# Second close of a four-stage transformer: last unit in halves, gate products in fp32r parts, clamps on GpSimd

## The reference

```python
# third stage, its end: out is the attention's output
gated = out @ w_gate + b_gate            # 256 -> 512
a, g = jnp.split(gated, 2, axis=-1)
x = x + a * jax.nn.sigmoid(g)
# fourth stage
y = _layernorm(x)
x_q = jnp.clip(y / input_scale, -448.0, 448.0)
x_dq = x_q.astype(jnp.float8_e4m3fn).astype(x.dtype) * input_scale
w_dq = weight_fp8 * weight_scale
x = x + jnp.einsum('bsi,oi->bso', x_dq, w_dq) + bias
```

## Time and profile before

| | |
|---|---|
| median of 3 runs | 2159.44 us (2157.16 to 2160.05) |
| profiled execution | 2158.82 us, its span 2157.1 us |
| PE / DVE / ACT / POOL busy in the span | 91% / 55% / 64% / 37% |
| second close | from about 2050 us to the end of the span |
| granted TensorE clock, mean | 0.95 |

### The profile page before, as it was taken

The page is one execution under the profiler, slowest core; times in us unless marked ns, Lnnn a source line. Parts: engine busy times, 40 slices in busy tenths (PEclk is TensorE's granted clock), DMA queues, the critical chain, the costliest instruction groups (busy, mean ns, idle before and its releaser), DMA issues. The chain is left out here.

```text
span 2157.1 us, 37876 instructions
## 1 busy us (share of the span) xinstructions
PE 1965.9 (91%) x12227; PEld 1132.6 (53%) x12227; DVE 1179.3 (55%) x2115; ACT 1384.8 (64%) x1585; POOL 804.5 (37%) x706
## 2 busy tenths in 40 slices
PE   6989999999956599999999999958899999999897
PEld 5722333323232488888888888857622222222255
DVE  5511163534557723323333333337599999999967
ACT  5689999999933233233233233226599999999943
POOL 2001010111120241443342444211078888988922
PEclk9989999999965699999999999979899999999999
DMA  6753243442210530202202220238944425463011
GB/s 207 232 97 69 46 102 59 107 71 60 59 41 0 195 128 29 87 29 83 91 28 85 89 84 26 86 115 300 300 67 106 94 53 117 59 151 63 27 63 70
DMA packets 76964, 203.63 MB, mean 94 GB/s; under 512 B 13092, under 2 KB 28262, under 8 KB 74664
## 3 DMA queue, kind: packets, MB, share of 16 engines
q1 hardware_dynamic: 67048, 179.26, 31.0%
q0 software_dynamic: 6816, 18.62, 2.5%
q10 hardware_dynamic: 2896, 3.16, 0.5%
HBM read 338.84 MB, written 60.03 MB: 185 GB/s over the span
## 5 line engine op out<-in xcount | busy, mean ns | idle before, releaser
L1291 PE MATMUL psum<-A_qa,A_ka 50*128 50x512 f32 x2048 | 417.7, 473 | 26.6 <-DVE A_qa L1375 7.3
L1291 PEld LDWEIGHTS psum<-A_qa,A_ka 50*128 50x128 f32 x2048 | 177.5, 186 | 476.9 <-DVE A1f_probs L1385 243.3
L2475 PE MATMUL psum<-e_w_high,e_xT 128*128 x1136 | 386.9, 402 | 3.9 <-DVE e_xT L2425 3.8
L1509 POOL TENSOR_TENSOR A1f_probs<-A1f_probs,A1f_bias 128x512 f32<-128x512 f32 x256 | 327.3, 1290 | 83.0 <-ACT A1f_probs L1343 82.6
L1331 ACT ACTIVATE A0f_probs<-psum 128x1024 f32<-128x1024 f32 x256 | 337.1, 1317 | 8.6 <-PE psum L1291 5.4
L1343 ACT ACTIVATE A0f_probs<-psum 128x1024 f32<-128x1024 f32 x256 | 338.5, 1322 | 0.0
L1385 DVE SCALAR_TENSOR_TENSOR A1f_probs<-psum,A1f_bias 128x1024 f32<-128x1024 f32 x256 | 311.7, 1218 | 24.0 <-PE psum L1291 20.7
L2432 DVE TENSOR_TENSOR e_hT<-psum,e_hT 128x1024 fp32r<-128x1024 f32 x71 | 87.0, 1225 | 421.3 <-ACT e_hT L2396 421.3
L1310 PE MATMUL psum<-A1f_probs,v 128*32 128x512 f32 x2048 | 274.4, 607 | 17.3 <-POOL A1f_probs L1509 15.8
L1335 ACT ACTIVATE A1f_probs<-A1f_probs 128x1024 f32<-128x1024 f32 x256 | 273.9, 1070 | 4.7 <-DVE A1f_probs L1385 3.8
L1310 PE MATMUL psum<-A0f_probs,v 128*32 128x512 f32 x2048 | 273.6, 606 | 0.0
(11 more groups left out here) (291 smaller groups left out, 2746.6 us busy)
## 6 DMA issues: line engine op xcount, KB each, us to landing
e_w_raw<-in_experts SPq DMA_DIRECT2D x73, 3072.0 KB, 11.5
qk_parts<-L_part SPq DMA_DIRECT2D x64, 512.0 KB, 3.9
A_qa<-qk_parts SPq DMA_DIRECT2D x192, 128.0 KB, 4.1
A_ka<-qk_parts SPq DMA_DIRECT2D x192, 128.0 KB, 6.1
om<-results SPq DMA_DIRECT2D x16, 512.0 KB, 8.6
A1f_bias<-tables SPq DMA_DIRECT2D x16, 384.0 KB, 8.5
A1f_bias<-tables SPq DMA_DIRECT2D x16, 320.0 KB, 10.4
L_x<-in_x SPq DMA_DIRECT2D x8, 512.0 KB, 6.6
```

The costliest lines, as they stand in the source:

```text
L1291: mm = e.matmul(ps[:, side * HALF:(side + 1) * HALF], self.qk.ka[rows, s, pair, kt * P:(kt + 1) * P].bitcast(FP32R), self.qk.qa[rows, s, p ...
L1509: e.tensor_tensor(fourth, fourth, self.bias_of(*w[1:], slice(self.FOURTH, GH)).rearrange("p h q -> p (h q)"), ALU.mult).then_inc(self.mult ...
L2475: mm = e.matmul(out, left[part].bitcast(FP32R), moving.bitcast(FP32R), start=start and i == 0, stop=stop and i == 2)
```

## The change

Three things in the second close. The last unit is cut in two halves of two tiles (`PIECES`): what comes after its statistics and root (rows, clamp, exponents, step, rounding, turn, copy, product, add, store) goes by pieces. ScalarE's order around the end is changed: the copy of unit 6 comes ahead of the steps of unit 7, and VectorE adds unit 5 ahead of unit 7's exponents. From unit 2 on (`PARTED`) the gate products are three fp32r products of parts for each of the two blocks, six for a tile instead of two plain fp32 ones; GpSimd makes the parts of the weights and of every unit, with three buffers. The clamps of units 0 to 6 move from VectorE to GpSimd. GpSimd also waits for all products of the attention before the stage, since its new buffers lie where the attention's were. Two semaphores are shared between the closes, with counts to match.

```diff
+    PARTED, PART_BUFS = 2, 3
+    PIECES = (*((u, 0, 4) for u in range(NT // 4 - 1)), (NT // 4 - 1, 0, 2), (NT // 4 - 1, 2, 4))
...
     def gate_pe(self, e, job):
...
+        if u >= self.PARTED and i == 0:
+            e.wait_ge(self.parted, self.parted_before + u - self.PARTED + 2)
...
+    def products(self, u, tile):
+        for k in range(DC):
+            if u < self.PARTED:
+                yield self.omT[:, k, u * self.W:(u + 1) * self.W][:, tile], self.wg[:, k, :]
+            else:
+                s = u % self.PART_BUFS
+                for om, w in ((self.om_high, self.wg_high), (self.om_high, self.wg_low), (self.om_low, self.wg_high)):
+                    yield om[:, s, k, tile].bitcast(FP32R), w[:, k, :].bitcast(FP32R)
...
     def act(self, e):
...
+            if u != n + 1:
+                for i in moved:
+                    self.moved_act(e, i)
+            for i in rows:
+                self.rows_act(e, i)
+            if u == n:
+                for i in self.of_unit(n - 2):
+                    self.moved_act(e, i)
             if u < n:
                 self.sigmoid_act(e, u, 1)
+            for i in rows:
+                self.step_act(e, i)
...
     def dve(self, e):
...
+            if u >= n:
+                for i in out:
+                    self.add_dve(e, i)
+            for i in behind:
+                self.exponents_dve(e, i)
             if u < n:
                 self.gate_dve(e, u, 1)
                 self.measure_dve(e, u)
+                for i in out:
+                    self.add_dve(e, i)
+            for i in behind:
+                self.round_dve(e, i)
...
+    def exponents_dve(self, e, n):
+        steps, y = self.m.dve, self.rows_of(n)
+        if n < self.UNITS - 1:
+            e.wait_ge(self.clamped, n + 1)
+        else:
+            e.wait_ge(self.normed, n + 1)
+            a = steps.of(e.tensor_scalar(y, y, FP8_MAX, -FP8_MAX, ALU.min, ALU.max))
+            e.wait_ge(steps.sem, a)
+        e.tensor_scalar(self.steps_of(n).bitcast(I32), y.bitcast(I32), 0x7F800000, None,
                         ALU.bitwise_and).then_inc(self.exponents, 1)
...
     def pool(self, e):
         self.m.pool.of(e.memset(self.power[:, :], -0.5))
+        self.wait_weights(e)
+        e.wait_ge(self.turned, 4 * B)
+        self.part(e, self.wg_high[:, :, :], self.wg_low[:, :, :], self.wg[:, :, :])
+        self.part_pool(e, self.PARTED)
         for u in range(self.UNITS):
             self.root_pool(e, u)
+            if u < self.UNITS - 1:
+                self.clamp_pool(e, u)
+            if u + self.PARTED + 1 < self.UNITS:
+                self.part_pool(e, u + self.PARTED + 1)
+
+    def part(self, e, high, low, whole):
+        steps = self.m.pool
+        a = steps.of(e.tensor_copy(high.bitcast(FP32R), whole))
+        e.wait_ge(steps.sem, a)
+        e.tensor_tensor(low.bitcast(FP32R), whole, high, ALU.subtract).then_inc(self.parted, 1)
+
+    def part_pool(self, e, u):
+        s = u % self.PART_BUFS
+        if u >= self.PARTED + self.PART_BUFS:
+            e.wait_ge(self.gate_full, 2 * (u - self.PART_BUFS + 1))
+        self.part(e, self.om_high[:, s, :, :], self.om_low[:, s, :, :], self.omT[:, :, u * self.W:(u + 1) * self.W])
+
+    def clamp_pool(self, e, u):
+        y = self.xn[:, u % self.BEHIND, :, :]
+        e.wait_ge(self.normed, u + 1)
+        e.tensor_scalar(y, y, FP8_MAX, -FP8_MAX, ALU.min, ALU.max).then_inc(self.clamped, 1)
...
                 if layer:
+                    self.fast[1].wait_products_done(e)
                     self.second_close.pool(e)
```

More of the change, by code:

```diff
@@ L712, in parts, with parted_before @@
         return [("part", 2 * b + half, c) for c in range(DC) for half in range(2)]
+    def parted_before(self):
+        return 1 + sum(len(self.parts(b)) for b in range(B))
     def heavy(self, u):
@@ L2575, in pe_order, with of_unit @@
                     order.append(("gate", u, i))
-                if before >= 0:
-                    order.append((kind, before))
-        return order
+                order.extend((kind, piece) for piece in self.of_unit(u - self.BEHIND))
+        return order
+    def of_unit(self, u):
+        return [i for i, piece in enumerate(self.PIECES) if piece[0] == u]
     def allocate_weights(self, sb):
@@ L2646, in sync @@
                         self.x2_src[a:z, :, :, :].rearrange("u p t d -> p u t d")).then_inc(self.x_in[i], DMA)
[L2647 to L2650, removed]
+        for n, (u, a, z) in enumerate(self.PIECES):
+            e.wait_ge(self.added, n + 1)
+            e.dma_start(self.out_dst[u, :, a:z, :], self.x[:, u, a:z, :]).then_inc(self.out_done, DMA)
+        e.wait_ge(self.out_done, DMA * len(self.PIECES))
     def pe(self, e):
@@ L2655, in pe @@
         for job in self.pe_order():
-            kind, u = job[0], job[1]
+            kind, n = job[0], job[1]
             if kind == "gate":
@@ L2659, in pe, with turn @@
             elif kind == "xq":
-                e.wait_ge(self.rounded, u + 1)
-                self.turn(e, job, self.xn[:, u % self.BEHIND, :, :], self.xq_full)
+                e.wait_ge(self.rounded, n + 1)
+                self.turn(e, job)
             else:
-                e.wait_ge(self.xq_moved, u + 1)
+                e.wait_ge(self.xq_moved, n + 1)
                 self.product_pe(e, job)
-    def turn(self, e, job, src, full):
-        ps = self.m.wide(self.ring.slot(job))
+    def turn(self, e, job):
+        u, a, z = self.PIECES[job[1]]
+        ps, w = self.m.wide(self.ring.slot(job)), (z - a) * P
         self.ring.wait_empty(e, job)
         for c in range(DC):
[L2670 to L2673, removed]
+            for t in range(a, z):
+                tr = e.transpose(ps[:, c * w + (t - a) * P:c * w + (t - a + 1) * P],
+                                 self.xn[:, u % self.BEHIND, t, c * P:(c + 1) * P], self.m.ident[:, :])
+        tr.then_inc(self.xq_full, 1)
     def gate_pe(self, e, job):
@@ L2735, in rows_act @@
             e.wait_ge(self.xq_full, u - self.BEHIND + 1)
-        for t in range(self.TILES):
+        for t in range(a, z):
             row = e.activation(self.xn[:, u % self.BEHIND, t, :], self.x[:, u, t, :], ACT.Identity,
@@ L2934, in __init__ @@
         sb.close()
[L2935 removed]
+        self.second_close = SecondClose(m, om, t, x2_dram, out_dram, self.close)
         self.second_close.allocate_weights(second)
```

99 lines of the change are left out of this document (49 added, 50 removed).

## The result

The changed kernel takes 2167.17 us (median of 7 runs, 2165.95 to 2171.74), the kernel before, beside it, 2159.44 (7 runs, 2157.16 to 2161.89). The ratio is 1.0038, with a 95% interval of 1.0027 to 1.0049: slower by 6 to 11 us. The forecast was 2173.0. The time is inside the range, 2158 to 2178, and at the low end of the forecast's own, 2167 to 2178. The forecast was 13.6 us above the kernel before, the time is 7.7 above it. The profiled execution took 2167.45 us with a span of 2165.7; before it was 2158.82 and 2157.1.

The account below looks back on a forecast made before the run. The bound was taken to be the latency circle of statistics, root, rows, clamp and exponents. Terms +14.0, +3.5, +0.8, -4.1, -0.3 gave +13.9 on 2158.82, 2172.7; adjusted towards the runs' median, forecast 2173.0 us, range 2158 to 2178.

Parts of the forecast that it names:

- What bounds the close: Second close: the latency circle of statistics, root, rows, clamp and exponents sets the pace, 10.16 us a unit.
- TensorE's products, nothing: Gate products from unit 2: fp32r saves 1.6 us of TensorE a unit, costed at nothing since off the circle.
- Parts, +14.0: Units 0 to 4: GpSimd's copy and subtraction hold VectorE's exponents and gate sum, 2.8 us a unit, five times.
- Clamps, +3.5: Units 0 to 6: the clamp on GpSimd takes 1.2 us plus a semaphore instead of 0.73, +0.5 each.
- Beginning, +0.8: After the last transpose: GpSimd's parts of the weights and unit 2 delay unit 0's second gate sum, +0.8 us.
- Tail, -4.1: Last statistics to last add: halves shorten 19.4 us to 15.3 with a half clock, -4.1 us.
- if the product of unit 6 runs at half clock again: Tail: TensorE idles about as long as before (4.6 us), so unit 6's product takes 1.7 us more, 15.3.
- Last store, -0.3: Span's end: the half-size last store behind an earlier store shortens its flight by perhaps 0.3 us.
- Rival 1: Circle: exponents get in ahead of GpSimd's copy, costing 0.8 to 1.9 a unit; 2163 to 2168 us; chance 0.18.
- Rival 3: Circle: VectorE's stopped instructions lose only about half of the predicted hold; 2155 to 2164 us; chance 0.12.
- Rival 4: Circle: GpSimd's long instructions don't stop VectorE, and root off the rounding takes 2.6 us; 2151 us; chance 0.15.
- Rival 2: Middle of the close: TensorE's clock drops, gates of 3 us take 6; 2174 to 2178 us; chance 0.05.

Follow-up runs that it names:

- Experiment 4: Changed kernel, but TensorE takes plain fp32 products in all units; GpSimd makes all parts and nobody reads them; 2168.55 us, ratio 1.0046.
- experiment 9: Kernel before plus last-unit halves, next first gate product ahead of rounding, negated mean behind power, VectorE waiting for the root; 2152.88 us, ratio 0.9970.
- experiment 2: Changed kernel without parts: plain fp32 products in all units, last-unit halves and GpSimd clamps kept; 2158.84 us, ratio 0.9996.
- Experiments 1: Changed kernel cut to last-unit halves and the new end order: plain fp32 products, no parts, clamps on VectorE; 2157.29 us, ratio 0.9983.
- 10: Kernel with last-unit halves alone (plain fp32 products, no parts, clamps on VectorE), measured once more; 2158.18 us, ratio 0.9989.
- experiment 7: Changed kernel with the last unit in one piece instead of halves; 2170.76 us, ratio 1.0044.
- experiment 5: Changed kernel, but GpSimd waits for VectorE's exponents of a unit before making parts; 2161.93 us, ratio 1.0006.
- experiment 11: Changed kernel with plain fp32 products everywhere and GpSimd's rounding and subtraction replaced by three constant fills, none read; 2165.31 us, ratio 1.0023.
- experiments 3: Changed kernel with clamps back on VectorE, so parts stand right behind the root on GpSimd; 2162.69 us, ratio 1.0009.
- 6: Changed kernel with the parts ahead of the clamp on GpSimd, right behind its root; 2165.05 us, ratio 1.0017.
- 8: Kernel before plus last-unit halves, next first gate product ahead of VectorE's rounding, negated mean behind GpSimd's power, no wait for the root; 2159.33 us, ratio 0.999.

## Why the prediction was right, point by point

**What bounds the close** (the circle of latencies) held: TensorE got cheaper products, and the time of the close rose by what the circle rose, less what the tail gave back. Experiment 4 shows the term "TensorE's products, nothing" to 0.1 us, and experiment 9 that plain products fit into a circle of 9.81 too. A gate job of two tiles now starts its 14 products 0.23 us apart (first 2134.40, last 2137.46), as worked out from the earlier trace rows.

**Parts, +14.0: mechanism right, mis-sized; measured +11.1** (85.43 - 74.31), and 11.4 with the beginning. This is the term that was furthest off. Per unit 2.28 for 2.8. The walk had the exponents end 1.65 behind the clamp's end and the subtraction 4.15; they ended 1.53 and 3.78 behind. Half of the error is in the subtraction, 2.25 behind the exponents' end where I had 2.5. I had taken it from a sum beside other work (2.45 and 2.66), while alone it takes 2.37, and its record of 2.70 overlaps the time in which VectorE finished the exponents. The gate sum and what follows it took 0.55 and 1.72 behind that, where I had 0.70 and 1.65. The prediction also said that a trace agreed for copies; its rows have only a sum and subtractions, and the copy's hold is first shown by the 1.50 row.

**Clamps, +3.5: measured +2.8** (experiment 2). The clamp lasts 1.04 us and not 1.2, as long as the rounding to parts over the same 1024: the two-step row that reads its factors from memory was the wrong neighbour, the copy the right one. The estimate of 0.9 us that the prediction also gave is 0.14 too low.

**Beginning, +0.8: measured +0.24.** GpSimd ended its first two pairs 7.49 us behind the last transpose (2059.54), at the near end of my 7.4 to 7.9; I had taken the far one. The second gate sum, begun at 2059.16, ended 0.55 behind that and was held for 0.24.

**Tail, -4.1: measured -5.64.** The walk to 13.6 was right (13.76 measured). The step that failed is "if the product of unit 6 runs at half clock again": the half clock fell on unit 5's product, off the path. Its premise failed too: TensorE idled 1.98 us before unit 6's product, not 4.6. Experiments 1 and 10 show the other branch, after the same 1.98: with the half clock on unit 6's product the stretch is 15.12 and 16.16, where the walk gave 15.3.

**Last store, -0.3: measured +0.6.** The last add's end to the span's end was 4.03 to 4.70 us in the eleven traces with halves, and 4.10 before and 4.38 in experiment 7 with a whole last unit: half the bytes bought nothing, and what moves it by 0.6 stays open.

Together the terms came to 9.1 us in place of 13.9, and 0.5 less ahead of the close makes 8.6. All terms but the last store were forecast too high, which is why the time fell at the low end; only the last store pulled the other way, by 0.9.

**Rival 1** did not happen as the changed kernel is written (the rounding to parts was first, by 0.08 us), but experiment 5 makes it happen, and it costs 0.7 a unit where I had 0.8 to 1.9. **Rival 3**, part of the hold, gave 2155 to 2164; the rows say that the hold is whole and the pieces a little smaller. **Rival 4** is refuted by the 1.50 and 2.16 rows, and its other half, that the root leaves the rounding and takes 2.6, came true only when experiment 9 made VectorE wait. **Rival 2**: no low clock from 2100 to 2120 (1.00). Unit 0's product, from 2085.15, did run at 0.50, after 4.83 us of idling, but the circles of units 1 and 2 are longer than the later ones by the same 0.6 as before, so it cost nothing.

Of the Trainium skill's rule on the shared port pair ("SBUF — State Buffer", the section on the two separate sides) the traces agree for the exponents, clamps and gate sums beside GpSimd's copies and subtractions, in both directions (2.16 us beside GpSimd's 2.70; GpSimd's first rounding of unit 2's parts 1.50 in place of 1.04, behind a gate sum). The page excepts a VectorE instruction with two SBUF inputs beside a GpSimd instruction that only writes, and there the trace agrees as well (0.69 under fills, experiment 11). For the 1.04 us power they do not agree, since VectorE's rounding starts 0.60 before it ends (2127.14 against 2127.74) and keeps its 1.21.

## What to carry to other kernels

Before work is given to GpSimd, ask which VectorE instructions will meet it, and what waits for them: the TensorE time saved here was free anyway (experiment 4), and 3.8 us a unit on GpSimd (2120.01 to 2123.84) cost 2.3 on the path. Where two engines hold each other, the order in which they start decides: one wait that lets the critical engine go first took 7.6 of 11.1 us off the circles, and one that keeps the long instruction off a chain of tiny ones made the fastest kernel. Cost a change's parts apart; here the one that pays (-3.2 to -4.3 us in the profiles) was hidden under two that don't.

## What the runs showed of the hardware that I had not expected

- Fills on GpSimd that read nothing hold VectorE's exponents all the same: 2.30 us in place of 0.69 (experiment 11). They don't hold the gate sum, which keeps 0.69 beside them.
- GpSimd's power over 128x4 is long (1.04 us) and lets VectorE's add and rounding run at 1.19 and 1.21 beside it, but when a rounding and the power both start at 2121.73, the rounding keeps 1.21 and the power is stretched to 2.11 (experiment 5).
- A GpSimd instruction that is next in its queue gets in ahead of a VectorE one that has yet to be told: 0.08 us decided 7.6. A VectorE instruction that waits already can get in between two of GpSimd's, but not always. In the changed kernel the gate sum of 2055.33 went in ahead of the rounding to parts recorded at 2055.61. In experiment 11 the exponents, there from 2119.97, were held through the fill of 2119.88 and the next one, and got in only ahead of the third, before which GpSimd waits. What makes the difference stays open.
- Even the root's first two instructions over 128x4, 0.23 us otherwise, take 1.11 and 1.18 in unit 2 of the kernel before, where VectorE's rounding starts at 2082.08 and they at 2082.26 and 2083.44. That is why the circles of units 1 and 2 are 10.77 and 10.74, where the prediction took 10.16 for all.
- TensorE's half clock fell on different products of the same tail (0.41 us a matmul, 0.28 at the full clock). In the changed kernel and experiments 3, 4, 5, 6, 7 and 11 it was unit 5's, after 3.94 to 4.36 us of idling, and unit 6's ran at the full clock. In the kernel before and experiments 1, 9 and 10, with 1.11 to 1.50 idle before unit 5's, it was unit 6's. In experiments 2 and 8, with 3.08 and 4.20 idle before unit 5's, it was both. And unit 7's whole product, after 1.11 of idling both times, had the full clock in the kernel before and the half clock in experiment 7. So the idling just before a product doesn't tell which.
